# Where the edge chunks lie beside the sort: 31 projected tiles ahead of them, and six chunks behind the last tile

## The reference

```python
h = relu(layernorm(x))
q, k, v = (h@Wq+bq)*scale, h@Wk+bk, h@Wv+bv          # per head
s = einsum('ehd,ehd->eh', q[src], k[dst])
p = exp(s - segment_max(s, src)[src]); attn = p / segment_sum(p, src)[src]
x = x + segment_sum(attn * v[dst], src) @ Wo + bo
h = relu(layernorm(x))
aggr = segment_sum(edge_attr, dst)                   # dst is sorted, src is not
x = x + relu(relu(concat(h, aggr)@W1+b1)@W2+b2)@W3+b3
```

## Time and profile before

| what | us |
|---|---|
| three runs | 1818.63, 1839.51, 1836.78 |
| their median | 1836.78 |
| the profiled execution, its time | 1829.74 |
| its span | 1827.1 |
| PE, DVE, ACT, POOL busy in the span | 1497.5, 1304.5, 906.2, 941.4 |
| mean granted clock of TensorE (1 is 2.4 GHz) | 0.902 |
| the first turn, the last half turn | 162.97, 324.46 |
| the first gather, the first multiply of the main loop | 324.39, 348.32 |

### The profile page before, as it was taken

How to read it: one execution, slowest core, us unless ns; L and a number is a source line. 1 busy time by engine, 2 the same in 40 slices (tenths; PEclk the granted TensorE clock), 3 DMA queues, 4 the chain that set the end, 5 groups by cost and what they waited for, 6 DMA issues and landing times.

```text
span 1827.1 us, 25716 instructions
## 1 busy us (share of the span) xinstructions
PE 1497.5 (82%) x7133; PEld 913.5 (50%) x7133; DVE 1304.5 (71%) x1999; ACT 906.2 (50%) x2865; POOL 941.4 (52%) x993
## 2 busy tenths in 40 slices
PE   4999989377878777887778877767888998998997
PEld 4544545244545444554445554434555655555654
DVE  9999998566777667776667776667766776776721
ACT  5844445264555455554455555522444554444553
POOL 6032544565665556655555566556655655665200
PEclk8999999678988898988888899888898999999998
DMA  9533667787888888878888888867667776777331
GB/s 219 112 115 128 216 210 236 218 308 265 303 286 267 272 285 280 298 272 282 283 259 279 280 284 291 273 196 230 207 205 223 230 226 203 215 229 231 110 105 33
DMA packets 217494, 418.69 MB, mean 229 GB/s; under 512 B 57816, under 2 KB 130719, under 8 KB 217343
## 3 DMA queue, kind: packets, MB, share of 16 engines
q0 software_dynamic: 68832, 225.25, 38.3%
q1 hardware_dynamic: 124569, 112.35, 20.4%
q10 hardware_dynamic: 23942, 79.35, 12.5%
HBM read 370.37 MB, written 46.38 MB: 228 GB/s over the span
## 4 chain that ended last, share of the span: by engine, by line
PE 22%; DVE 20%; ACT 19%; another core or an unknown queue 18%; issue 15%; SPq 3%; DMA 3%; ACTq 1%; DVEq 0%
PE bank L1720 5%; ACT EBO L1171 5%; ACT EBO L1179 4%; DVE U L2039 4%; DVE V L2533 3%; DVE U L2040 3%; PE bank L1536 3%; DVE V L2592 2%; DVE V L2542 2%; PE bank L1795 2%; PE bank_pair L1704 2%; PE bank L1821 2%; PE bank L1805 1%; PE bank_pair L1740 1%
## 5 line engine op out<-in xcount | busy, mean ns | idle before, releaser
L986 POOL DMA_INDIRECT U<-kv_rows,dstb x856 | 813.1, 950 | 568.3 <-issue 241.1
L1720 PE MATMUL bank<-V 128*128 128x264 f32 x1712 | 475.8, 419 | 18.3 <-issue 11.1
L1720 PEld LDWEIGHTS bank<-V 128*128 128x128 f32 x1712 | 346.0, 207 | 111.8 <-issue 45.9
L2533 DVE TENSOR_TENSOR V<-U,bank_pair 128x1024 f32<-128x1024 f32 x214 | 259.9, 1214 | 161.3 <-issue 67.3
L1171 ACT ACTIVATE EBO<-iota,dA 128x64 f32<-128x64 f32 x692 | 228.5, 340 | 175.9 <-remote 95.3
L2592 DVE TENSOR_TENSOR V<-U,bank 128x1024 f32<-128x1024 f32 x214 | 259.1, 1211 | 50.1 <-ACT bank L1307 40.0
L1704 PE MATMUL bank_pair<-V 128*128 128x256 f32 x428 | 164.2, 469 | 139.5 <-issue 126.9
L1536 PE MATMUL bank<-EBO 128*64 128x256 f32 x1568 | 251.4, 413 | 27.8 <-DMA EBO<-in_edge_attr_dram 14.6
L2542 DVE TENSOR_REDUCE V<-V 128x32 f32<-128x1024 f32 x214 | 259.5, 1213 | 2.1
L1179 ACT ACTIVATE EBO<-EBO,ones 128x64 f32<-128x64 f32 x600 | 208.8, 348 | 32.0 <-remote 7.8
L1704 PEld LDWEIGHTS bank_pair<-V 128*128 128x128 f32 x428 | 75.1, 211 | 219.3 <-issue 201.9
(11 more groups left out here) (297 smaller groups left out, 2032.0 us busy)
## 6 DMA issues: line engine op xcount, KB each, us to landing
EBO<-in_edge_attr_dram ACTq DMA_DIRECT2D x147, 512.0 KB
EBO<-in_edge_attr_dram SPq DMA_DIRECT2D x48, 512.0 KB
U<-kv_rows,dstb POOLq DMA_INDIRECT x856
kv_rows<-U SPq DMA_DIRECT2D x49, 256.0 KB, 2.0
ag_rows<-R SPq DMA_DIRECT2D x196, 64.0 KB
V<-q_rows SPq DMA_DIRECT2D x54, 128.0 KB
w_rows<-V SPq DMA_DIRECT2D x54, 128.0 KB
V<-slot_places SPq DMA_DIRECT2D x52, 128.0 KB
```

Of the source, the lines that this page charges most:

```text
L986: e.indirect_dma_start(out=kvb[:, b % n, j, :], out_offset=None, in_=kv_dram[:, :], in_offset=bass.IndirectOffsetOnAxis(ap=dstb[:, k:k + 1 ...
L1720: t = e.matmul(o[:, 0:RW], ohog[b % NPV], PVg[b % NPV][:, j, :, :].rearrange("p h d -> p (h d)"), start=first and j == 0, stop=y == SG - 1 ...
L2533: e.tensor_tensor(Tg, kvb[:, b % NKG, :, 0:D], qv, ALU.mult).then_inc(b_mult, 1)
```

## The change

One number: the rule lets chunks in only from the 32nd projected tile on, where before it was the 27th.

```diff
@@ -415,7 +415,7 @@
         AGG_STEPS = 8 * NCH
         LQ = NQ - 1
         LAG = SG
-        ALONE = ET + 21
+        ALONE = ET + 26
         NOH = 4
         SEAM = 8
```

## The result

The changed kernel takes 1842.88 us (median of 20 runs), the kernel before 1830.28 on the same chip (20 runs): ratio 1.0064, 95% interval 1.0045 to 1.0083. One of the changed kernel's runs, 1866.73 us, was in a slower state of the chip and is left out of the ratio; the plain difference of the two medians is 12.6. The forecast was 1841, +9.3 us in its sum. The profiled execution took 1841.29, with a span of 1839.5 and a mean granted clock of 0.916.

The account below looks back on a forecast made before the run. DVE's sort was taken as the bound, PE nearly one. Half turn 11.5 + 1.0 + 1.0 = 13.5 us later, less 4.2 given back, made +9.3 (6.6 to 13.0); on a 1831.2 mean, 1841 us, range 1826 to 1856.

Parts of the forecast that it names:

- Levels 11 to 17: Sort turns beside moved tiles: DVE waits more at level 11, part returns at level 12; +1.0 us carried (0.3 to 2.6).
- The third rival: Second turns of levels 12 to 17 lose their cover, PE arriving late: 11.4 us on top, +20.7, 1852; chance 0.12.
- Six chunks in a row: Level 17: SP takes 5.0 us per chunk where PE wants 1.95, so the half turn ends 11.5 us later.
- the clock: Level 17: PE idles before each spaced chunk and may run at the low clock; +1.0 us (0 to 1.9).
- The first two rivals: Level 17: SP does not pace the chunks, 1828, chance 0.13; or half of it, only SP's issues count, 1834, chance 0.13.
- POOL's one-hots: Level 17: POOL's four per chunk stay hidden by the edge loads, with 0.6 us to spare.
- The gathers: Loop start: q rows land early, so the first gather waits for indices alone; 13.5 later less 4.2 given back, 9.3 us.
- the setup moves by the same 13.5: Behind the last half turn: DVE's setup shifts as much as the first half turn, from 343.8 to 357.3 us.
- both chains end together: Main loop start: gathers allow the first multiply at 357.6 us and the setup at 357.3, the loop behind unchanged.
- first gather + 23.9: Main loop start: the first multiply comes a fixed 23.9 us after POOL's first gather, as in the trace before.

Follow-up runs that it names:

- no border rows by SP: The changed kernel without SP's two small writes F <- R in the chunks 16 to 21; ratio to the kernel before 1.0045, +8.2 us.
- four chunks behind the last tile: The changed kernel with ALONE = ET + 24 instead of ET + 26, so four edge chunks follow the last tile instead of six; ratio 1.0047, +8.5 us.
- gathers late: The changed kernel with POOL's first gather held until DVE has written the loop's register values; ratio to the kernel before 1.0088, +15.9 us.
- gathers behind the half turn: The changed kernel with POOL's first gather held until the second half's node numbers are written, behind the last half turn; ratio 1.0085, +15.4 us.
- the last half turn late: The kernel before with 24 repeats of a small DVE operation ahead of the last half turn; ratio 1.0009, +1.6 us.
- before, gathers late: The kernel before with POOL's first gather held until DVE has written the loop's register values; ratio 1.0016, +2.9 us.
- loads by ACT: The changed kernel with the loads of edge chunks 18 to 23 issued from ACT's queue instead of SP's; ratio to the kernel before 1.0066, +12.0 us.

## Why the prediction was right, and where it was not

**Levels 11 to 17: right, a little high.** I carried +1.0 to level 17. The last second turn moved by 2.5, of which 2.1 were there at the first turn: +0.4. At the second turn of level 12 it was still 0.9; the rest came back on the way. The low clock did come to the first of the four tiles, as the range allowed (granted clock 0.68 from 168.7 to 174.0, its first pair of matmuls 2.07 us instead of 1.13). The third rival, turns that lose their cover, didn't happen.

**Six chunks in a row: right.** The forecast was 11.5 from SP's queue and 1.0 from the clock, 12.5; it is 24.69 - 12.00 = 12.7. The steps were 4.94, 5.02 and 5.09 us for the forecast 5.0, and the load of chunk 21 stood 16.5 behind the turn (16.1). From there PE was 0.5 faster at its data than the 5.5 taken and 1.3 slower in the last 14 matmuls (3.25 for 1.94), where I had put half of 1.9. The low clock came to three of the five chunks that stood behind an idle PE, not to all of them, and not to the half turn (0.66). That SP is the cause is shown: 1.2 us of issues less in its queue shorten the step by 0.9, another issuer takes 5.8 off, and with four chunks instead of six the stretch is in between. The first two rivals are out by the same rows. POOL's one-hots, four to a chunk, were hidden as I said: PE's waits in the row all end with a load.

**The gathers: right.** The first was released by DVE's indices and came 11.3 later, 9.2 without the 2.1; the forecast was 9.3.

**The setup and the first multiply: wrong.** The step that failed is "the setup moves by the same 13.5", and with it "both chains end together". The last half turn came 15.2 us later, 13.1 without the 2.1, which is near the forecast. But the flag came 25.0 us later (354.38 against 329.40): the other 9.8 are the two waits of DVE, 3.5 and 7.0 where they were 0.5 and 0.2. The setup's last piece ended at 365.8 instead of 343.8, and the first multiply followed it at 366.6, not at 356 to 360. That is 30.9 us behind the first gather instead of 23.9. The sum had no term for a setup that takes longer beside gathers. The second of DVE's two waits (ahead of `nqi`) was 3.1 to 7.0 us in six of the nine kernels whose first gather stands 2.3 us or more ahead of the last half turn, and 0.4, 1.2 and 1.3 in the other three; in the three kernels that hold the gathers behind that turn it was 0.21 each time. So in these traces, one of each kernel, an early start of the gathers goes with it and is not enough for it. What DVE waits for there, the trace doesn't name; that its instructions come late behind gathered rows is argued, not shown, and the cause stays open. The Trainium skill, "Runtime: NRT & Kernel Launch", "Instruction fetch mechanics", calls the fetch of straight code mostly hidden; no run here could prove or refute that this was one.

**The first multiply as the end of the sum: wrong, and the sum near by luck.** I took it to be first gather + 23.9 and all behind it as unchanged. From first gather to first multiply the traces show 15.3 to 35.5 us. By my own rule the measured first multiply would have meant +18.3. It didn't, because behind it the changed kernel took 1472.9 us and not 1478.8, and the rows show where these 5.9 lie. Before, DVE waits 3.1 and 1.7 us for gathered rows ahead of the second and third multiply, and the fifth stands 19.5 us behind the first. In the changed kernel no multiply from the second to the fifth waits for rows, and it is 13.5. So there the fifth hangs on the late setup, and not on the gathers, which the sum had taken as its term. That the gathers' 9.2 and the fifth multiply's 10.2 lie close is no proof that one made the other. In "no border rows by SP" and "four chunks behind the last tile" the first gather was 2.8 and 3.5 us sooner than in the changed kernel and the fifth multiply was not (+10.9, +10.5). With the gathers held ("gathers late", "gathers behind the half turn") it was later (+13.8, +16.0). From the first gather to the fifth multiply it is 43.5 us before, 44.4 in the changed kernel, 44.1 with the last half turn late, 41.6 to 42.8 with gathers held, and 46.3 to 49.3 in the other seven kernels, which start them early. At the pace of the kernels whose first rounds did wait for gathered rows, the fifth multiply of the changed kernel would stand at 377 to 379 (an estimate: 335.71 + 41.6 to 43.5); it came at 380.15. The two chains lie 1 to 3 us apart there, and that is why a sum with the wrong one ended near the measured 11.7.

**The time.** The sum had +9.3 with 6.6 to 13.0, the measurement 11.7 with 8.2 to 15.2. The difference of 1.5 between the fifth multiply's 10.2 and the time is below what these runs resolve. A single trace tells about the start of the loop, and only the medians about the whole: with "before, gathers late" the last multiply came 22 us earlier than before though the fifth was level. Some 16 of these 22 are what the two chips differ by (1830.28 and 1814.62 for the same kernel), and single executions of the kernel before on one chip spread over more than 20 us (1799.70 to 1822.78).

## What to carry to other kernels

Count the steps of the queue that feeds a stretch, not only the engine's work in it: a chunk was 1.95 us for PE and 5.0 for SP, and it was free only as long as tiles that need little of SP stood between. When a chain ends at the first instruction of a buffered loop, read the shift a few rounds in, where buffers have levelled out: there it was 10.2 where the first round said 16.2. Then ask again which waits lie ahead of it: before, the rounds in between waited for gathered rows, and in the changed kernel none did. Transfers that may start earlier need not start the loop sooner: what is set up beside them may come later, and from first gather to fifth multiply it then took up to 6 us longer.

## What the hardware did that I had not expected

- 1.2 us taken from the issues of one queue shortened a step from 5.0 us to 4.2 (three steps of each trace), though that queue had stood with no wait named by the trace.
- With the DMA engines full (share 1.04, 412 GB/s from 343 to 347) DVE stood 3.5 and 7.0 us in a piece of setup, 6.0 of the 7.0 for something that the trace doesn't name. With the gathers held until its first part was done ("gathers behind the half turn") the same piece ran with waits of 0.5 and 0.2. Full engines alone don't do it: before, with share 1.00 and 363 GB/s beside it, it was 0.5 and 0.2 as well.
- Late steps beside early gathers are not DVE's alone: in "loads by ACT" DVE's two waits were 0.5 and 1.3, but SP's first load of q rows stood 21.9 us behind the flag (359.26, 337.36), where it was 4.6 before.
- The low clock came and went inside the row: 14 matmuls of one chunk took 3.19, the next 1.94, the next 2.89, then 3.25, and the last 1.94, each behind idle times of 0.2 to 2.4 us. The granted clock was 0.71, 0.94, 0.76, 0.56 and 1.00 in the five stretches.
